# One kernel, an attention layer and a mixture of experts: seven statements moved in the step that joins its two halves

## The reference, cut to what matters

```python
logits = x @ router_w.T
top_vals, top_idx = jax.lax.top_k(logits, TOP_K)          # TOP_K = 1
...
gate_up = jnp.einsum('eth,ehf->etf', xr, gate_up_proj)
gate, up = jnp.split(gate_up, 2, axis=-1)
routed = jnp.einsum('etf,efh->eth', up * jax.nn.silu(gate), down_proj)
shared = jax.nn.silu(x @ shared_gate_w) * (x @ shared_up_w) @ shared_down_w
```

## Time and profile before

| | |
|---|---|
| median of 3 runs | 549.22 us (548.59 to 549.43) |
| the profiled execution's own time | 548.71 us |
| its span, first to last instruction | 546.9 us |
| PE busy | 535.1 us (98%) |
| DVE busy | 406.1 us (74%) |
| POOL busy | 337.6 us (62%) |
| ACT busy | 229.0 us (42%) |
| mean granted PE clock | 0.996 of full speed |

### The profile page before, as it was taken

The page is one execution under the profiler, slowest core; times in us unless marked ns, Lnnn a source line. Parts: engine busy times, 40 slices in busy tenths (PEclk is TensorE's granted clock), DMA queues, the critical chain, the costliest instruction groups (busy, mean ns, idle before and its releaser), DMA issues. The chain is left out here.

```text
span 546.9 us, 11803 instructions
## 1 busy us (share of the span) xinstructions
PE 535.1 (98%) x3832; PEld 452.2 (83%) x3832; DVE 406.1 (74%) x891; ACT 229.0 (42%) x410; POOL 337.6 (62%) x330
## 2 busy tenths in 40 slices
PE   8999999999999999999999999999999999999995
PEld 6777887888888888888787688888888888888884
DVE  5896987887887887987877688666866666666664
ACT  4445552553552552552543765133333333333331
POOL 1956676673783575784574576437776656556644
PEclk9999999999999999999999999999999999999998
DMA  7930508307606206404464914856677666565651
GB/s 253 328 111 3 192 3 142 129 1 173 214 1 189 83 2 131 141 0 155 156 233 149 354 38 155 324 149 191 192 179 197 192 202 199 164 196 191 198 183 39
DMA packets 46554, 83.82 MB, mean 153 GB/s; under 512 B 11360, under 2 KB 30576, under 8 KB 46480
## 3 DMA queue, kind: packets, MB, share of 16 engines
q1 hardware_dynamic: 38720, 64.52, 37.9%
q0 software_dynamic: 6112, 15.40, 10.3%
q10 hardware_dynamic: 1664, 3.15, 1.6%
HBM read 61.11 MB, written 22.34 MB: 153 GB/s over the span
## 5 line engine op out<-in xcount | busy, mean ns | idle before, releaser
L1753 PE MATMUL duo<-w_gu_hi,xsT 128*128 x320 | 107.2, 397 | 0.0
L1753 PE MATMUL duo<-x1T,wsgu 128*128 128x512 f32 x366 | 86.8, 392 | 0.4 <-DVE hT L1298 0.4
L1753 PEld LDWEIGHTS duo<-x1T,wsgu 128*128 128x128 f32 x366 | 68.1, 188 | 14.9 <-DVE hT L1298 0.9
L1162 POOL DMA_INDIRECT out_rows<-of,seat x39 | 39.5, 1014 | 56.5 <-DVE of L1710 54.3
L1753 PEld LDWEIGHTS duo<-w_gu_hi,xsT 128*128 128x128 f32 x320 | 59.7, 188 | 11.2
L1753 PE MATMUL duo<-w_gu,xsT 128*128 x160 | 62.0, 388 | 0.0
L1663 DVE SCALAR_TENSOR_TENSOR eh<-duo,seat,e_act 128x512 f32<-128x512 f32 x38 | 28.5, 751 | 40.1 <-PE duo L1753 40.1
L988 POOL TENSOR_TENSOR turned<-turned,swapped 128x1024 f32<-128x1024 f32 x16 | 38.5, 2406 | 29.1 <-DVE swapped L1226 29.1
L1235 DVE TENSOR_TENSOR sims<-duo,causal 128x512 f32<-128x512 f32 x64 | 41.0, 683 | 15.7 <-ACT sims L727 15.7
L1153 POOL DMA_INDIRECT xz<-xz_d,seat x39 | 45.5, 1166 | 8.9 <-issue 8.7
L727 ACT ACTIVATE sims<-duo 128x256 f32<-128x256 f32 x64 | 21.1, 382 | 64.2 <-PE duo L1833 64.0
(11 more groups left out here) (220 smaller groups left out, 1295.0 us busy)
## 6 DMA issues: line engine op xcount, KB each, us to landing
dn_rest<-dn_lo_d SPq DMA_DIRECT2D x39, 512.0 KB
w_gu<-L_ffn_gate_up_proj SPq DMA_DIRECT2D x8, 1024.0 KB, 8.2
x_in<-x_t SPq DMA_DIRECT2D x8, 512.0 KB, 7.1
x_res<-L_attn_x SPq DMA_DIRECT2D x8, 512.0 KB, 4.0
dn_raw<-L_ffn_down_proj SPq DMA_DIRECT2D x8, 512.0 KB, 8.4
dn_hi_d<-dn_top SPq DMA_DIRECT2D x8, 512.0 KB, 5.9
dn_lo_d<-dn_low SPq DMA_DIRECT2D x8, 512.0 KB, 6.5
xz_d<-zs SPq DMA_DIRECT2D x8, 512.0 KB
```

The source lines that it names most:

```text
L1162: pool.indirect_dma_start(out, bass.IndirectOffsetOnAxis(ap=seat[:, s, 1:2], axis=0), of[:, s % OUTS, :], None).then_inc(sig.out_done[s % ...
L1753: last = mm(out_, left(a, k), right(b, k), start=start and k == 0 and n == 0, stop=stop and k == kt - 1 and n == len(PASSES) - 1)
```

## The change

Five things move; no instruction is added, taken away or changed in size.

- **PE:** `rank`, `y_transposes(7)` and `output(7)` stand behind whole column blocks: rank and y behind both blocks of j = 2, the output behind both blocks of j = 3.
- **ACT:** the high half of expert 3 goes from ahead of the silus to behind that of j = 1; `y_scaled(7)` goes behind the silu of j = 2; the high halves of experts 2, 1 and 4 come behind the silu of j = 3.
- **DVE:** the low half of expert 0 goes from ahead of pair 6's products to behind the shared sums, directly ahead of the low half of expert 2. The product of j = 3 goes ahead of the output sums.
- **POOL:** `norm_scales(7)` goes ahead of the last of pair 6's four scatters.

```diff
@@ ACT
                 if has(f):
-                    if t == PAIRS:
-                        expert_hi(3)
...
                     if t == PAIRS:
-                        y_scaled(a)
-                        expert_hi(2)
+                        expert_hi(3)
                     shared_act(f, 2)
                     h_high(f, 2)
                     if t == PAIRS:
-                        expert_hi(1)
+                        y_scaled(a)
                     shared_act(f, 3)
                     h_high(f, 3)
                     if t == PAIRS:
+                        expert_hi(2)
+                        expert_hi(1)
                         expert_hi(4)
@@ POOL
                 for q in range(TILES):
+                    if p == PAIRS - 2 and q == TILES - 1:
+                        norm_scales(p + 1)
                     seat_scatter(p, q)
...
-                if t == PAIRS:
-                    norm_scales(a)
@@ DVE
                     x1_lo(f)
                     variance(a)
-                    expert_lo(0, 2)
...
                         shared_product(f, 2)
+                        shared_product(f, 3)
                         for i in range(2):
                             output_sum(a, [i])
...
-                    shared_product(f, 3)
+                    if t < PAIRS:
+                        shared_product(f, 3)
...
                     if t == PAIRS:
+                        expert_lo(0, 2)
                         expert_lo(2, 4)
@@ PE
                     gate_up_shared(f, 2, 0)
+                    gate_up_shared(f, 2, 1)
+                    if t <= PAIRS:
+                        rank(f)
                     if t == PAIRS:
-                        rank(f)
                         y_transposes(a)
-                    gate_up_shared(f, 2, 1)
-                    if t < PAIRS:
-                        rank(f)
                     gate_up_shared(f, 3, 0)
+                    gate_up_shared(f, 3, 1)
                     if t == PAIRS:
                         output(a)
-                    gate_up_shared(f, 3, 1)
```

## The result

The changed kernel takes 554.82 us (median of 4 runs, 554.25 to 555.27), the kernel before 549.18 (4 runs, 548.59 to 549.43). The ratio is 1.0103, 95% interval 1.0091 to 1.0115: 5.6 us slower, against a forecast of 554.7. The profiled execution took 554.25 us with a span of 552.4; its mean granted clock is 0.993 where before had 0.996.

The account below looks back on a forecast made before the run. PE, busy 98% of the span, bounds the kernel. A net 4.3 us delay at pair 7's block (2, 0) plus 1.25 us of clock gives +5.5: 554.2 us profiled, 554.7 us median; range 549.9 to 556.8.

Parts of the forecast that it names:

- Step 8's gain: PE from pair 6's products to x1's transposes: earlier product and scales start pair 7's first block 1.02 us earlier, at 329.97.
- The moved low half: DVE behind the shared sums: expert 0's low half adds 2.23 us, eating the 1.02 us gain even undisturbed.
- the undisturbed case: DVE and POOL don't hinder each other: PE goes on at 336.35 at pair 7's block (2, 0), 0.07 us ahead.
- POOL in between: POOL's subtraction for expert 5 runs between DVE's two low halves, inferred from a scatter's row; block (2, 0) starts at 340.72.
- the +4.3: Delay in us of pair 7's block (2, 0) on PE against 336.42, with POOL let in between DVE's subtractions.
- The clock: PE's clock falls to half speed in the 4.9 us wait ahead of pair 7's block (2, 0), costing 1.25 us.
- 2.5 us after PE stopped: When PE's clock falls in the wait, taken from the fall at the end of the span.
- As long as the fall took: How long PE's clock stays down after the wait: 2.5 us of work at half speed, costing 1.25 us.
- The clock staying up: Rival: PE's clock stays full through the wait in pair 7, only +4.3 us, 553.5 us; chance 0.12.
- DVE keeping its turn: Rival: DVE's second subtraction follows the first, POOL waits, `expert_lo(1)` stands, down product 1.1 us late: 550.3 us; chance 0.10.
- Nothing hinders: Rival: POOL and DVE run side by side, PE 0.07 us ahead at block (2, 0): 549.1 us; chance 0.08.
- faster: Rival: the change does what it says and PE keeps its 1.02 us: 548.2 us; chance 0.03.

Follow-up runs that it names:

- Experiments 5 and 6: 5: the changed kernel with expert 0's low half and POOL's scales put back, 549.18 us; 6: the kernel before with only POOL's scales moved, 548.65 us.
- experiment 7: The changed kernel with POOL's subtraction for expert 5 held back until DVE has done the low halves of experts 3, 0 and 2: 551.66 us.
- experiment 3: The changed kernel with POOL's subtraction for expert 5 cut into two instructions of 1024 columns each: 552.31 us.
- experiment 4: The changed kernel with 20 matmuls, results unused, ahead of block (2, 0) of pair 7 to keep PE at work: 552.93 us.
- experiment 2: The kernel before with only expert 0's low half moved behind the shared sums on DVE: 555.82 us.

## Why the prediction was right, step by step

**Step 8's gain.** Right in place and size. No wait of PE at block (2, 0) of pair 6, the projection unmoved at 317.96, the down product at 321.52 (forecast 321.54), pair 7's first block at 329.97 (forecast 329.97). Experiments 5 and 6 confirm that the scales bound it: without them earlier, PE's lead ends in a wait.

**The moved low half.** Right: it costs more than the gain even undisturbed. With POOL held back (experiment 7) the pair took 4.48 us, and block (2, 0) started at 336.27 where 336.35 was forecast for the undisturbed case: PE's lead of 1 us was spent in a gap of 0.88.

**POOL in between.** Right: the +4.3 us measured 4.23. The order, POOL ahead of DVE's second subtraction, showed in the change, and cutting POOL's instruction in two halved the loss. But the row that the step rested on doesn't show a turn taken from DVE: in the earlier trace rows the two DVE instructions that ran beside the scatter took 1.36 us together, where the one of their size ahead of them took 0.69 alone. The choice between the two orders was thus luck in part; only its price was worked out from rows of two subtractions. The Trainium skill ("SBUF — State Buffer", section "Who interferes with whom") has the port held for a whole instruction; the turns of experiment 3 agree, with 2.17 us lost to a half and 4.33 to the whole.

**The clock.** The mechanism was right, its size a little small and its timing wrong. The term was 1.25 us; the profiled execution shows 1.4, and between the medians of the change and experiment 4 it is 1.9. The four runs of the change fall into 554.25 and 554.47 (mean clock 0.993 and 0.994) and 555.16 and 555.27 (0.991, as in all four runs of experiment 2), and only one of the first two was profiled. The step "2.5 us after PE stopped" didn't hold: PE's last weight load ended at 335.09, its last matmul 0.4 us later, and the clock fell at 340.1, 4.6 us after that; by the same reading it was 3.0 us in experiment 2 and 3.7 in experiment 3. "As long as the fall took", 2.5 us of work at half speed, was 3.1 us of work here (340.36 to 343.5) and 5.0 in experiment 2 (341.27 to 346.3). That the forecast is within 0.2 us of the median is in part luck, since this term could have come out at 2.2.

**The rivals.** The clock staying up (553.5) occurred in neither profile of the 5 us wait; with PE kept at work (experiment 4) it gives 552.9. DVE keeping its turn (550.3) didn't occur; forced, it costs 551.7, as the rival had left out the gathers behind POOL's instruction. "Nothing hinders" and "faster" fall with the 8.84 us. The gain that the last one names exists, but only with the low half left where it was.

What stays open is what decides whether the clock falls after a gap of some 3 us, and how long it then stays down.

## What to carry to other kernels

Price a moved instruction at its new neighbours, not only by its length: a subtraction of 2.3 us between SBUF tensors, put ahead of another beside POOL's, cost a whole POOL instruction (4.3 us) and then PE's clock (1.4 to 1.9). Where one engine is busy all the time, list what each other engine must finish before its next block, and count there the slack that a move uses. Test the parts of a reordering alone and together: here the loss sat in one line, two other parts gave a gain clear of the noise only together, and putting that line back made the best kernel, 547.9 us.

## What the runs showed of the hardware that was not expected

- The turns between DVE and POOL were forecast, but no row of before showed them for two subtractions. With POOL waiting and DVE holding two subtractions in a row, POOL went in between in every trace in which they met so (the change, and experiments 2 to 4); with POOL's work in two instructions the turns alternated.
- The clock can fall after PE has resumed: in experiment 3 work began again at 338.34, and full clock ended at about 339.4.
- Time at half clock isn't fixed: about 3.4 us in the change (340.1 to 343.5) and in experiment 3 (339.4 to 342.8), about 6.8 us in experiment 2 (339.4 to 346.3), with PE at work during most of it.
